# One ring of three PSUM banks for scores, diagonal blocks and turned maxima, drained by ScalarE, and value products of two steps back to back

## The chip, the cores and the metric

The kernel runs on one core of a Trainium2 chip. The metric is the device time of one execution, in microseconds (us). The engines are called TensorE (PE, with PEld for its weight loads), VectorE (DVE), ScalarE (ACT), GpSimd (POOL) and SyncE (SP, which starts most transfers).

## The reference, cut to what matters

A transformer block on 8 sequences of 1024 rows and 256 columns: a modulated layer norm, attention, a second modulated layer norm, and a feed-forward part whose operands are rounded to four bits in blocks of 16. The change touches attention alone:

```python
k_rec, v_rec = up-projections of latent_kv      # 16 heads of 16 columns
scores = einsum('bhqd,bhkd->bhqk', qh, k_rec) / sqrt(d)
scores = scores * exp(-0.01 * abs(q - k))       # a decay that depends on the distance
attn = softmax(scores, axis=-1)
out = einsum('bhqk,bhkd->bhqd', attn, v_rec)
```

The softmax subtracts each row's maximum of the decayed scores, so a maximum must be known before the exponentials are taken.

## The kernel before, in words

Four stages follow each other: setup, projection, attention (`attend_stage`, lines 494 to 985) and the feed-forward part. Projection leaves q and k in two scaled versions ("low" and "up"), each split into three bf16 parts, so that six bf16 terms stacked on 96 partitions make an exact enough fp32 product. Above the diagonal one version carries the decay, below it the other. The 128x128 block on the diagonal fits neither, and is made apart.

Attention works in 32 units, one for each sequence and group of four heads. A unit has 16 steps: `g // 8` is the half of the 1024 queries, `g % 8` the block of 128 keys. Everything is written out as one fixed order for each engine. Engines meet through counting semaphores.

TensorE, `unit_steps` (793 to 808), in each step:

- `scores` (744) four times, one for each head h: 128 keys by 512 queries. In a diagonal step (8 of 16: g = 0 to 3 and 12 to 15) the 128 queries of the diagonal block are left out, which leaves 384.
- Between them two tiles of `max_tile` (724), four matmuls: the scores of a later unit, 128 queries by 1024 keys, for the row maxima. The order in a step is S0, A first half, S1, A second half, B first half, S2, B second half, S3. Below, S0 to S3 are the score products and A and B the two tiles of a step; in the second step of a pair of steps the tiles are called C and D.
- After S1, where the next step is a diagonal one, `diagonals` (765): four 128x128 products into `side_ps`.
- At the end `values` (777) of the step two back (`LAG = 2`): four heads side by side in four column groups of 32 of the array, fp32, which the trace records as eight matmuls.
- After step 9, `turn_maxima` (737): two transposes of the maxima of the next unit, also into `side_ps`.

The maxima tiles have two buffers, `max_ps[:, i % 2]`, of two banks each. `bank_was_free` (565) lets the first half of tile i start when VectorE has finished tile i - 2. The scores have two banks, `score_ps[:, i % 2]`; `side_ps` and `pv_ps` have one each. That is all eight banks.

VectorE (`maxima`, 891) multiplies each tile with the decay and takes the row maximum, in one custom instruction and a short read of the result. In steps 7 and 8 it splits the maxima into three bf16 parts (901), in step 10 it copies the turned maxima (919). In the last two units it multiplies the diagonal block by its decay (927), reading `side_ps`.

ScalarE, `unit_steps` (860), takes the exponential of each score bank (`exp`, 839; on the diagonal steps with g % 4 of 1 or 2 over all 512 columns, those of the diagonal block among them). After h = 1 it takes the exponential of the diagonal block of the step before (`diagonal_exp`, 854), after h = 3 it copies the next diagonal block out of `side_ps` (`copy_diagonal`, 847), and twice a unit it copies the output (`copy_out`, 832). GpSimd multiplies the copied diagonal block by its decay (691) and subtracts the maxima (699). `probs` has four buffers, and `exp` of step g waits for `values` of step g - 4.

SyncE loads the operands of later units and waits for the events of this order (636).

Of the kernel before, what the change touches and what calls it, by code (L numbers as in the profile page):

```python
# [26 lines left out]
ALU = mybir.AluOpType  # L27
# [466 lines left out]
def attend_stage(nc, ctx, t, w):  # L494
# [12 lines left out]
    DIAG_EXP = 1  # L507
    LATE = UNITS * B - 2
# [6 lines left out]
    def sem(name):  # L515
# [27 lines left out]
    turned_max = side_ps[0:3 * UH * TILES, 0, 0:P // 2].bitcast(BF16)  # L543
    turned_whole = side_ps[0:UH * TILES, 1, :]
# [11 lines left out]
    max_turn_ready, max_turn_copied = sem("max_turn_ready"), sem("max_turn_copied")  # L556
    scores_ready, pv_done = sem("scores_ready"), sem("pv_done")
    diag_ready, diag_copied, diag_decayed, diag_shifted, diag_exp_done = (
        sem("diag_ready"), sem("diag_copied"), sem("diag_decayed"), sem("diag_shifted"), sem("diag_exp_done"))
    out_copied = sem("out_copied")  # L560
    out_stored = [sem(f"out_stored{i}") for i in range(OUTS)]
    maxima_done, exp_done = sem("maxima_done"), sem("exp_done")
    block = st.enter_context(nc.Block())

    def bank_was_free(eng, done, unit, per_unit, i):
# [19 lines left out]
    def tiles_of(b, u, g, last):  # L585

        later = 1 if g < STEPS // 2 else 2
        if last and later == 1 or isinstance(b, int) and UNITS * b + u + later >= UNITS * B:
            return None
        first = (g * PER_STEP + AHEAD) % MAX_TILES  # L590
        return (b, u + later, first) if u + later < UNITS else (b + 1, (u + later) % UNITS, first)

    @block.sync
    def _(sp):
# [41 lines left out]
        def step(unit):  # L636
            nonlast = unit < UNITS * B - 1
            if unit > 0:

                sp.wait_ge(exp_done, SCORE_TILES * unit)  # L640
                sp.wait_ge(diag_copied, 2 * DIAG * unit)
# [12 lines left out]
            if unit + 3 < UNITS * B:  # L654
                load_low((unit + 3) // UNITS, (unit + 3) % UNITS)
# [26 lines left out]
    @block.gpsimd  # L682
    def _(pool):
        for i in range(UNITS):
            nc.gpsimd.memset(low[1][i][KROWS:KROWS + 3], -1.0).then_inc(minus_ones_set, 1)
        for i in range(2):
            nc.gpsimd.memset(up[1][i][KROWS:KROWS + 3], -1.0).then_inc(minus_ones_set, 1)
        pool.wait_ge(const_loaded, 16)
        pool.wait_ge(minus_ones_set, UNITS + 2)

        def decay_diagonal(unit, g):
            n = diagonals_before(unit, g)
            pool.wait_ge(diag_copied, n + 1)
            if n > 0:
                pool.wait_ge(diag_shifted, n)
            nc.gpsimd.tensor_tensor(diag[:, g % 2], diag[:, g % 2], diag_decay[:].unsqueeze(1).broadcast_to([P, UH, P]),  # L696
                                    ALU.mult).then_inc(diag_decayed, 1)

        def shift_diagonal(unit, g):
            n, hf, at = diagonals_before(unit, g), g // TILES, g % DIAG * P  # L700
            pool.wait_ge(diag_copied if unit >= LATE else diag_decayed, n + 1)
            if n > 0:
                pool.wait_ge(diag_shifted, n)
            pool.wait_ge(shift_loaded[hf], 16 * (unit + 1))
            nc.gpsimd.tensor_tensor(diag[:, g % 2], diag[:, g % 2], shift[:, hf, :, at:at + P],  # L705
                                    ALU.subtract).then_inc(diag_shifted, 1)

        def unit_steps(unit):
            for g in range(DIAG):
                if unit < LATE:  # L710
                    decay_diagonal(unit, g)
                shift_diagonal(unit, g)
            for g in range(TILES + DIAG, STEPS):
                if unit < LATE:
                    decay_diagonal(unit, g)
                shift_diagonal(unit, g)

        for unit in range(UNITS * B):
            unit_steps(unit)
    @block.tensor  # L720
    def _(pe):
        pe.wait_ge(ident_ready, 1)

        def max_tile(b, u, i, half):
# [12 lines left out]
        def turn_maxima(unit):  # L737
            pe.wait_ge(max_parts_ready, 3 * (unit + 1))
            if unit > 0:
                pe.wait_ge(diag_copied, 2 * DIAG * unit - DIAG)  # L740
            pe.transpose(turned_max, max_parts[:].rearrange("p t n -> p (t n)"), ident_bf[:])
            pe.transpose(turned_whole, row_max[:, unit % 2], w["ident"][:]).then_inc(max_turn_ready, 1)

        def scores(b, u, g, h):

            hf, kb = g // TILES, g % TILES
            unit, i = UNITS * b + u, UH * g + h
# [6 lines left out]
            bank_was_free(pe, exp_done, unit, SCORE_TILES, i)  # L754
            if turn > q0:
                mm = pe.matmul(score_ps[:, i % 2, 0:turn - q0], up[1][u % 2][:, h, ks],  # L756
# [3 lines left out]
            if q1 > turn:  # L760
                mm = pe.matmul(score_ps[:, i % 2, turn - q0:HALF], low[1][u][:, h, ks],  # L761
                               low[0][u][:, h, turn:q1], start=True, stop=True)
            mm.then_inc(scores_ready, 1)

        def diagonals(b, u, g):
# [3 lines left out]
            if g == 0 and unit == 0 or g == TILES + DIAG and unit < UNITS * B - 1:  # L769
                pe.wait_ge(max_turn_copied, 2 * (unit + 1 + (g > 0)))  # L770
            pe.wait_ge(diag_copied, diagonals_before(unit, g))
            for h in range(UH):
                mm = pe.matmul(side_ps[:, h, :], low[1][u][0:KROWS, h, ks], low[0][u][0:KROWS, h, ks],  # L773
                               start=True, stop=True)
            mm.then_inc(diag_ready, 1)

        def values(b, u, g):
# [9 lines left out]
            pe.wait_ge(exp_done, SCORE_TILES * unit + UH * (g + 1))  # L787
# [5 lines left out]
        def unit_steps(b, u, first, last):  # L793
            unit = UNITS * b + u
            for g in range(STEPS):
# [9 lines left out]
                if not (first and g < LAG):  # L805
# [25 lines left out]
    def _(act):  # L831
# [7 lines left out]
        def exp(unit, g, h):  # L839
            i = UH * g + h  # L840
            first = P if is_diagonal(g) and g % DIAG == 0 else 0
            end = HALF - P if is_diagonal(g) and g % DIAG == DIAG - 1 else HALF
            act.wait_ge(scores_ready, SCORE_TILES * unit + i + 1)
            nc.scalar.activation(probs[:, g % PROBS, h, first:end], score_ps[:, i % 2, first:end],  # L844
                                 ACT.Exp).then_inc(exp_done, 1)

        def copy_diagonal(b, u, g):
            n = diagonals_before(UNITS * b + u, g)
            act.wait_ge(diag_ready, n + 1)
            if n >= 2:  # L850
                act.wait_ge(diag_exp_done, n - 1)
            nc.scalar.activation(diag[:, g % 2], side_ps[:], ACT.Copy).then_inc(diag_copied, 1)  # L852

        def diagonal_exp(b, u, g):
            unit, at = UNITS * b + u, g % DIAG * P
            act.wait_ge(exp_done, SCORE_TILES * unit + UH * (g + 1))
# [30 lines left out]
    def _(dve):  # L887
# [31 lines left out]
        def copy_turned(unit):  # L919
            dve.wait_ge(max_turn_ready, unit + 1)  # L920
            dve.wait_ge(max_rows_loaded, 16 * 6 * unit)
            if unit > 0:
                dve.wait_ge(max_stored, 16 * unit)
            nc.vector.tensor_copy(max_turned[:], turned_max).then_inc(max_turn_copied, 1)
            nc.vector.tensor_copy(max_whole[:], turned_whole).then_inc(max_turn_copied, 1)

        def decay_diagonal(b, u, g):
            n = diagonals_before(UNITS * b + u, g)
            dve.wait_ge(diag_ready, n + 1)
            dve.wait_ge(diag_exp_done, n - 1)  # L930
            nc.vector.tensor_tensor(diag[:, g % 2], side_ps[:], diag_decay[:].unsqueeze(1).broadcast_to([P, UH, P]),  # L931
                                    ALU.mult).then_inc(diag_copied, 1)
# [6 lines left out]
        def round_weights(step):  # L939

            pieces = len(weights) * QUANT_STEPS
            for n in range(pieces * step // FREE_STEPS, pieces * (step + 1) // FREE_STEPS):
                if n == 0:
                    dve.wait_ge(weights_loaded, 16 * 5)
                    dve.wait_ge(exp_done, SCORE_TILES * (UNITS * (B - 1) + 1))
                    dve.wait_ge(diag_copied, 2 * DIAG * (UNITS * (B - 1) + 1))
# [5 lines left out]
        def unit_steps(b, u, last):  # L952
            unit = UNITS * b + u
            following = (b, u + 1) if u < UNITS - 1 else (b + 1, 0)
            for g in range(STEPS):
                ahead = tiles_of(b, u, g, last)
                for i in range(PER_STEP):
# [4 lines left out]
                    if not last and (g, i) == (10, 0):  # L962
                        copy_turned(unit + 1)
# [9 lines left out]
        copy_turned(0)  # L973
# [713 lines left out]
```

## Time and profile before

| | us |
|---|---|
| median of 3 runs | 2623.03 (2622.95 to 2626.25) |
| the profiled execution, its own time | 2628.24 |
| its span, first to last instruction | 2626.4 |
| busy TensorE, matmuls | 2451.9 (93%) |
| busy VectorE | 2078.3 (79%) |
| busy ScalarE | 1840.8 (70%) |
| busy GpSimd | 1290.8 (49%) |

The span is the time from the first to the last instruction on the core. The execution's own time is 1.8 us longer. A matmul's record reaches from its start to its modelled end, and matmuls overlap in the array, so TensorE looks busier than it is: the pitch from one start to the next tells its speed, not the length of a record. A record followed by "x2" covers two instructions. In brackets behind a record stands how long the engine sat idle before it and what released it.

### The profile page before, as it was taken

How to read it: one execution, taken by the hardware profiler on the slowest of the kernel's cores; microseconds unless marked ns; L12 is line 12 of the kernel's file. 1: busy time of each engine (PE TensorE's matmuls, PEld its weight loads, DVE VectorE, ACT ScalarE, POOL GpSimd, SP SyncE). 2: the span in 40 equal slices, each digit the busy share in tenths (PEclk: the TensorE clock that was granted, in tenths of full speed). 3: DMA queues.
4: the chain of work that ended last, by engine and by line, in shares of the span. 5: the costliest groups of instructions: out<-in, count | busy, mean ns of one | idle time of the engine just before them, and what ended most of it. 6: DMA issues, size and time to landing. Idle time of an engine off the chain costs nothing. (4 is left out here: it accounts for less than half of the span.)

```text
span 2626.4 us, 40901 instructions
## 1 busy us (share of the span) xinstructions
PE 2451.9 (93%) x12710; PEld 1034.0 (39%) x12710; DVE 2078.3 (79%) x3876; ACT 1840.8 (70%) x3608; POOL 1290.8 (49%) x1107
## 2 busy tenths in 40 slices
PE   5878759999999999999999999999886999999998
PEld 3333312333333333333333333333223666666665
DVE  5988878888888888888888888888755787888875
ACT  3666605888888888888888888888743555555554
POOL 3656642535435344353453543534314677777774
PEclk9677757999999999999999999999986999999999
DMA  4777884756647557466474564755302112212110
GB/s 151 240 249 246 266 162 133 149 117 138 142 97 159 120 122 159 98 142 138 110 163 105 137 143 98 162 117 113 88 25 66 51 57 57 57 55 57 57 45 18
DMA packets 273769, 315.54 MB, mean 120 GB/s; under 512 B 38032, under 2 KB 182160, under 8 KB 273424
## 3 DMA queue, kind: packets, MB, share of 16 engines
q1 hardware_dynamic: 264336, 304.54, 48.1%
q10 hardware_dynamic: 9216, 8.39, 0.9%
q8 instruction: 102, 1.67, 0.3%
q14 instruction: 115, 0.94, 0.1%
HBM read 225.78 MB, written 85.46 MB: 119 GB/s over the span
## 5 line engine op out<-in xcount | busy, mean ns | idle before, releaser
L897 DVE CUSTOM_DVE_ANT_0 unread<-max_ps,toeplitz_sb 128x1024 bf16<-128x1024 f32 x1024 | 1219.6, 1222 | 263.8 <-PE max_ps L732 260.0
L844 ACT ACTIVATE probs<-score_ps 128x512 f32<-128x512 f32 (+1 forms) x2048 | 1074.5, 589 | 207.7 <-PE score_ps L761 122.2
L732 PE MATMUL max_ps<-k_low,q_low 96*128 96x512 bf16 x2048 | 719.7, 393 | 27.4 <-DVE ident_bf L888 17.9
L696 POOL TENSOR_TENSOR diag<-diag,diag_decay 128x512 f32<-128x512 f32 x240 | 305.1, 1271 | 840.6 <-ACT diag L852 828.0
L789 PE MATMUL pv_ps<-probs,v 128*32 128x512 f32 x4096 | 546.9, 606 | 0.0
L756 PE MATMUL score_ps<-q_up,k_up 99*128 99x512 bf16 (+3 forms) x1280 | 411.1, 322 | 14.3 <-ACT probs L844 13.4
L761 PE MATMUL score_ps<-q_low,k_low 99*128 99x512 bf16 (+3 forms) x1280 | 406.6, 319 | 6.1 <-ACT probs L844 5.0
L705 POOL TENSOR_TENSOR diag<-diag,shift 128x512 f32<-128x512 f32 x256 | 334.1, 1305 | 86.0 <-DVE diag L931 66.1
L1335 PE MATMUL gu_ps<-wgu_t,turned 128*128 128x512 f32 (+1 forms) x768 | 316.3, 562 | 0.8 <-DVE hid L1550 0.8
L756 PEld LDWEIGHTS score_ps<-q_up,k_up 99*128 99x128 bf16 x1280 | 123.2, 97 | 458.9 <-ACT probs L844 434.0
L732 PEld LDWEIGHTS max_ps<-k_low,q_low 96*128 96x128 bf16 x2048 | 197.5, 98 | 188.0 <-DVE row_max L897 86.6
L348 POOL TENSOR_TENSOR parts<-rest,parts 128x512 bf16<-128x512 f32 x128 | 173.7, 1376 | 105.9 <-ACT parts L463 104.3
L761 PEld LDWEIGHTS score_ps<-q_low,k_low 99*128 99x128 bf16 x1280 | 124.5, 98 | 248.9 <-ACT probs L844 183.0
L852 ACT ACTIVATE diag<-side_ps 128x512 f32<-128x512 f32 x240 | 154.1, 642 | 73.9 <-PE side_ps L773 73.9
L1335 PEld LDWEIGHTS gu_ps<-wgu_t,turned 128*128 128x128 f32 x768 | 142.4, 192 | 142.4 <-issue 124.4
L1308 PE MATMUL fdown_ps<-wd_g,hid_t 128*128 128x256 f32 (+1 forms) x768 | 190.5, 390 | 4.8 <-DVE y_out L1570 3.9
L858 ACT ACTIVATE probs<-diag 128x512 f32<-128x512 f32 x256 | 171.1, 668 | 0.2 <-POOL diag L705 0.2
L1308 PEld LDWEIGHTS fdown_ps<-wd_g,hid_t 128*128 128x128 f32 (+1 forms) x768 | 141.4, 191 | 44.8 <-issue 21.8
L1360 ACT ACTIVATE turned<-fturn_ps 128x256 f32<-128x256 f32 x64 | 24.6, 384 | 177.3 <-PE fturn_ps L1325 177.3
L1550 DVE TENSOR_TENSOR hid<-gu_ps,silu 128x704 f32<-128x704 f32 x64 | 57.1, 892 | 110.6 <-ACT silu L1400 110.6
L789 PEld LDWEIGHTS pv_ps<-probs,v 128*32 128x32 f32 x4096 | 80.8, 108 | 123.2 <-issue 110.1
L305 DVE TENSOR_TENSOR rest<-full,parts 128x512 f32<-128x512 f32 x128 | 116.8, 922 | 15.6 <-ACT parts L459 9.4
(154 smaller groups left out, 2845.5 us busy)
## 6 DMA issues: line engine op xcount, KB each, us to landing
shift<-max_whole_dram SPq DMA_DIRECT2D x64, 1024.0 KB, 7.6
splits<-parts SPq DMA_DIRECT2D x128, 384.0 KB, 2.7
q_low<-splits SPq DMA_DIRECT2D x192, 128.0 KB, 7.1
k_low<-splits SPq DMA_DIRECT2D x192, 128.0 KB, 8.3
q_up<-splits SPq DMA_DIRECT2D x192, 128.0 KB, 9.3
k_up<-splits SPq DMA_DIRECT2D x192, 128.0 KB, 10.2
v_padded<-v_out SPq DMA_DIRECT2D x64, 256.0 KB, 3.7
v<-v_padded SPq DMA_DIRECT2D x32, 512.0 KB, 12.1
```

Source lines behind the costliest of these rows:

```text
L348: nc.gpsimd.tensor_tensor(parts[:, n % RING, 2, :], rest[:, n % RING, :], parts[:, n % RING, 1, :], ALU.subtract).then_inc(low_ready, 1)
L696: nc.gpsimd.tensor_tensor(diag[:, g % 2], diag[:, g % 2], diag_decay[:].unsqueeze(1).broadcast_to([P, UH, P]), ALU.mult).then_inc(diag_dec ...
L705: nc.gpsimd.tensor_tensor(diag[:, g % 2], diag[:, g % 2], shift[:, hf, :, at:at + P], ALU.subtract).then_inc(diag_shifted, 1)
L732: mm = pe.matmul(max_ps[:, i % 2, half * HALF:(half + 1) * HALF], low[0][u][0:KROWS, h, qb * P:(qb + 1) * P], low[1][u][0:KROWS, h, half * ...
L756: mm = pe.matmul(score_ps[:, i % 2, 0:turn - q0], up[1][u % 2][:, h, ks], up[0][u % 2][:, h, q0:turn], start=True, stop=True)
L761: mm = pe.matmul(score_ps[:, i % 2, turn - q0:HALF], low[1][u][:, h, ks], low[0][u][:, h, turn:q1], start=True, stop=True)
L789: mm = pe.matmul(pv_ps[h * VW:(h + 1) * VW, :], v[u % 2][:, kb, h, :], probs[:, g % PROBS, h, :], start=(kb == 0), stop=(kb == TILES - 1))
L844: nc.scalar.activation(probs[:, g % PROBS, h, first:end], score_ps[:, i % 2, first:end], ACT.Exp).then_inc(exp_done, 1)
L858: nc.scalar.activation(probs[:, g % PROBS, :, at:at + P], diag[:, g % 2], ACT.Exp).then_inc(diag_exp_done, 1)
L897: nc.vector.tensor_tensor_reduce(unread[:, i % 2, :], max_ps[:, i % 2, :], toeplitz[:, at:at + S], 1.0, -3.0e38, ALU.mult, ALU.max, row_ma ...
L1308: mm = pe.matmul(down_ps[:, 0:D], hid_t[i % 2][0:rows, c, :], w["wd_g"][0:rows, b, c, :], start=(c == 0), stop=(c == IC - 1))
L1335: mm = pe.matmul(gu_ps[:, c:min(c + HALF, GU)], turned[i % 2][:, k, :], w["wgu_t"][:, k, c:min(c + HALF, GU)], start=(k == 0), stop=(k == ...
```

## The change

One ring of three banks, `score_ps[:, at % 3]`, takes the place of the two score banks and of `side_ps`. `ring_order` lists everything that passes through it: the turned maxima of a unit, the diagonal blocks and the scores, in TensorE's order. `ring_ready` counts what TensorE has filled, `ring_drained` what ScalarE has emptied. A write to the ring waits for the entry three before it. ScalarE now drains every entry: it copies the diagonal block after h = 1, not after h = 3, and in the last two units too; it copies the turned maxima after step 9, in place of VectorE; its exponential in diagonal steps leaves the diagonal block out, as two instructions where that block lies inside; and it copies the output after h = 0 of steps 2 and 10, not after steps 1 and 9. On TensorE the value products of two steps stand together at the end of each odd step. The maxima tiles, their two buffers and their place between the scores are as before.

```diff
-    score_ps = st.enter_context(nc.psum_tensor("score_ps", [P, 2, HALF], F32))
-    side_ps = st.enter_context(nc.psum_tensor("side_ps", [P, UH, P], F32))
+    score_ps = st.enter_context(nc.psum_tensor("score_ps", [P, RING, HALF], F32))
...
+    def ring_order():
+        yield "turn", 0
+        yield "diagonal", 0, 0
+        for unit in range(UNITS * B):
+            for g in range(STEPS):
+                for h in range(UH):
+                    yield "score", unit, g, h
+                    if h == 1 and g < STEPS - 1 and is_diagonal(g + 1):
+                        yield "diagonal", unit, g + 1
+                    if h == 1 and g == STEPS - 1 and unit < UNITS * B - 1:
+                        yield "diagonal", unit + 1, 0
+                if g == 9 and unit < UNITS * B - 1:
+                    yield "turn", unit + 1
...
     @block.tensor
+        def ring_free(*tile):
+            at = ring_at[tile]
+            if at >= RING:
+                pe.wait_ge(ring_drained, at - RING + 1)
+            return at % RING
...
         def scores(b, u, g, h):
-            bank_was_free(pe, exp_done, unit, SCORE_TILES, i)
+            slot = ring_free("score", unit, g, h)
...
         def diagonals(b, u, g):
-            pe.wait_ge(diag_copied, diagonals_before(unit, g))
+            slot = ring_free("diagonal", unit, g)
...
         def values(b, u, g):
-            pe.wait_ge(exp_done, SCORE_TILES * unit + UH * (g + 1))
+            pe.wait_ge(ring_drained, ring_at["score", unit, g, UH - 1] + 1)
...
-                if not (first and g < LAG):
+                if g % 2 == 1 and not (first and g < LAG):
+                    values(*steps_back(b, u, g, LAG + 1))
                     values(*steps_back(b, u, g, LAG))
...
     @block.scalar
         def exp(unit, g, h):
-            first = P if is_diagonal(g) and g % DIAG == 0 else 0
-            end = HALF - P if is_diagonal(g) and g % DIAG == DIAG - 1 else HALF
+            block = g % DIAG * P
+            pieces = [(0, block), (block + P, HALF)] if is_diagonal(g) else [(0, HALF)]
+            act.wait_ge(ring_ready, at + 1)
+            for first, end in pieces:
+                if first < end:
+                    op = nc.scalar.activation(probs[:, g % PROBS, h, first:end], score_ps[:, at % RING, first:end],
+                                              ACT.Exp)
+            op.then_inc(ring_drained, 1)
...
         def copy_diagonal(b, u, g):
+            act.wait_ge(ring_ready, at + 1)
             if n >= 2:
                 act.wait_ge(diag_exp_done, n - 1)
...
+        def copy_turned(unit):
+            nc.scalar.activation(max_turned[:], bank[0:3 * UH * TILES, 0:P // 2].bitcast(BF16),
+                                 ACT.Copy).then_inc(max_turn_copied, 1)
+            nc.scalar.activation(max_whole[:], bank[0:UH * TILES, P:2 * P], ACT.Copy).then_inc(max_turn_copied, 1)
+            act.wait_ge(max_turn_copied, 2 * (unit + 1))
+            act.sem_inc(ring_drained, 1)
...
                 for h in range(UH):
                     exp(unit, g, h)
+                    if h == 0 and g == 2 and not first:
+                        copy_out(unit - 1, 1)
+                    if h == 0 and g == TILES + 2:
+                        copy_out(unit, 0)
                     if h == DIAG_EXP and not (first and g == 0) and is_diagonal((g - 1) % STEPS):
                         diagonal_exp(*steps_back(b, u, g, 1))
-                if is_diagonal((g + 1) % STEPS) and unit + (g == STEPS - 1) < LATE:
-                    copy_diagonal(*steps_on(b, u, g))
-                if g == 1 and not first:
-                    copy_out(unit - 1, 1)
-                if g == TILES + 1:
-                    copy_out(unit, 0)
+                    if h == 1 and is_diagonal((g + 1) % STEPS) and not (last and g == STEPS - 1):
+                        copy_diagonal(*steps_on(b, u, g))
+                if g == 9 and not last:
+                    copy_turned(unit + 1)
...
     @block.vector
         def decay_diagonal(b, u, g):
-            nc.vector.tensor_tensor(diag[:, g % 2], side_ps[:], diag_decay[:].unsqueeze(1).broadcast_to([P, UH, P]),
-                                    ALU.mult).then_inc(diag_copied, 1)
+            nc.vector.tensor_tensor(diag[:, g % 2], diag[:, g % 2], diag_decay[:].unsqueeze(1).broadcast_to([P, UH, P]),
+                                    ALU.mult).then_inc(late_decayed, 1)
```

## Rows read from the trace of the kernel before

**Rows 1.** The page: its first line.

```profile
span 2626.4 us, 40901 instructions
```

**Rows 2.** Windows: engines' busy us (instructions), PEclk, DMA share, GB/s.

```profile
1015.10:1062.50 47.40, 46.95 (x307) 15.81 (x305) 38.79 (x71) 40.74 (x82) 20.41 (x16) 1.00 0.60 130
1868.50:1920.00 51.50, 41.77 (x260) 11.80 (x258) 30.16 (x31) 40.27 (x80) 13.86 (x8) 0.97 0.18 51
```

**Rows 3.** Waits of the whole span: us in total, times, longest.

```profile
PEld score_ps L756 <- ACT probs L844: 434.0, 829, 1.7
...
PEld max_ps L732 <- DVE row_max L897: 86.6, 169, 1.5
```

**Rows 4.** Timeline of one ordinary step: start, length, engine, line, operation.

```profile
1000.12 0.39 PE L756 MATMUL score_ps<-q_up,k_up 99*128 99x512 bf16 x1
...
1000.61 2.16 ACT L844 ACTIVATE probs<-score_ps 128x512 f32<-128x512 f32 x4 [0.37 <-PE score_ps L756]
...
1000.78 0.59 PE L732 MATMUL max_ps<-k_low,q_low 96*128 96x512 bf16 x2
1001.25 0.10 PEld L756 LDWEIGHTS score_ps<-q_up,k_up 99*128 99x128 bf16 x1 [0.36 <-ACT probs L844]
...
1001.31 1.22 DVE L897 CUSTOM_DVE_ANT_0 unread<-max_ps,toeplitz_sb 128x1024 bf16<-128x1024 f32 x1 [0.57 <-PE max_ps L732]
...
1001.75 0.39 PE L756 MATMUL score_ps<-q_up,k_up 99*128 99x512 bf16 x1
...
1002.07 1.06 PE L789 MATMUL pv_ps<-probs,v 128*32 128x512 f32 x8
...
1002.46 1.22 DVE L897 CUSTOM_DVE_ANT_0 unread<-max_ps,toeplitz_sb 128x1024 bf16<-128x1024 f32 x1
...
1003.07 0.39 PE L756 MATMUL score_ps<-q_up,k_up 99*128 99x512 bf16 x1
```

**Rows 5.** Timeline: a maxima tile that waits for VectorE.

```profile
1005.75 1.22 DVE L897 CUSTOM_DVE_ANT_0 unread<-max_ps,toeplitz_sb 128x1024 bf16<-128x1024 f32 x1
...
1007.04 0.10 PEld L732 LDWEIGHTS max_ps<-k_low,q_low 96*128 96x128 bf16 x1 [0.48 <-DVE row_max L897]
```

**Rows 6.** Timeline of PEld at attention's end, where value products follow each other.

```profile
1932.55 0.13 PEld L789 LDWEIGHTS pv_ps<-probs,v 128*32 128x32 f32 x4 [0.30 <-ACT probs L858]
1932.98 0.13 PEld L789 LDWEIGHTS pv_ps<-probs,v 128*32 128x32 f32 x4 [0.30 <-issue]
```

**Rows 7.** Timeline: the split of the maxima, and the transposes of two units.

```profile
1010.21 1.22 DVE L897 CUSTOM_DVE_ANT_0 unread<-max_ps,toeplitz_sb 128x1024 bf16<-128x1024 f32 x1 [0.41 <-PE max_ps L732]
...
1011.56 1.22 DVE L897 CUSTOM_DVE_ANT_0 unread<-max_ps,toeplitz_sb 128x1024 bf16<-128x1024 f32 x1
...
1014.90 0.26 PE L741 MATMUL side_ps<-ident_bf,max_parts 128*96 128x128 bf16 x1
...
1062.44 0.26 PE L741 MATMUL side_ps<-ident_bf,max_parts 128*96 128x128 bf16 x1
```

**Rows 8.** Timeline of TensorE in diagonal steps 13 and 14 of a unit.

```profile
1024.80 0.59 PE L732 MATMUL max_ps<-k_low,q_low 96*128 96x512 bf16 x2
...
1027.10 0.28 PE L756 MATMUL score_ps<-q_up,k_up 99*128 99x256 bf16 x1
...
1027.66 0.59 PE L732 MATMUL max_ps<-k_low,q_low 96*128 96x512 bf16 x2
```

**Rows 9.** Timeline of ScalarE in diagonal steps, and one output copy.

```profile
1028.54 0.68 ACT L858 ACTIVATE probs<-diag 128x512 f32<-128x512 f32 x1
1029.06 1.14 ACT L844 ACTIVATE probs<-score_ps 128x512 f32<-128x512 f32 x2
1030.02 0.68 ACT L852 ACTIVATE diag<-side_ps 128x512 f32<-128x512 f32 x1
1030.49 0.96 ACT L844 ACTIVATE probs<-score_ps 128x384 f32<-128x384 f32 x2
...
1039.10 0.63 ACT L837 ACTIVATE out_t<-pv_ps 128x512 f32<-128x512 f32 x1
```

More of the change, by code:

```diff
@@ L507, in attend_stage @@
     DIAG_EXP = 1
+    RING = 3
     LATE = UNITS * B - 2
@@ L555, in attend_stage, with ring_order_table @@
         sem("max_scores_ready"), sem("max_parts_ready"), sem("max_rest_ready"))
[L556 to L559, printed above, removed]
+    max_turn_copied = sem("max_turn_copied")
+    ring_ready, ring_drained, pv_done = sem("ring_ready"), sem("ring_drained"), sem("pv_done")
+    diag_decayed, late_decayed, diag_shifted, diag_exp_done = (
+        sem("diag_decayed"), sem("late_decayed"), sem("diag_shifted"), sem("diag_exp_done"))
     out_copied = sem("out_copied")
     out_stored = [sem(f"out_stored{i}") for i in range(OUTS)]
-    maxima_done, exp_done = sem("maxima_done"), sem("exp_done")
+    maxima_done = sem("maxima_done")
     block = st.enter_context(nc.Block())
+    def ring_order_table():
+        return {tile: i for i, tile in enumerate(ring_order())}
     def bank_was_free(eng, done, unit, per_unit, i):
@@ L638, in step @@
             if unit > 0:
-                sp.wait_ge(exp_done, SCORE_TILES * unit)
-                sp.wait_ge(diag_copied, 2 * DIAG * unit)
+                sp.wait_ge(ring_drained, ring_at["score", unit, 0, 0])
                 load_shift(unit, 1)
@@ L692, in decay_diagonal @@
             n = diagonals_before(unit, g)
-            pool.wait_ge(diag_copied, n + 1)
+            pool.wait_ge(ring_drained, ring_at["diagonal", unit, g] + 1)
             if n > 0:
@@ L700, in shift_diagonal @@
             n, hf, at = diagonals_before(unit, g), g // TILES, g % DIAG * P
-            pool.wait_ge(diag_copied if unit >= LATE else diag_decayed, n + 1)
+            if unit < LATE:
+                pool.wait_ge(diag_decayed, n + 1)
+            else:
+                pool.wait_ge(late_decayed, n - 2 * DIAG * LATE + 1)
             if n > 0:
@@ L738, in turn_maxima @@
             pe.wait_ge(max_parts_ready, 3 * (unit + 1))
[L739 to L742, printed above, removed]
+            bank = score_ps[:, ring_free("turn", unit), :]
+            pe.transpose(bank[0:3 * UH * TILES, 0:P // 2].bitcast(BF16),
+                         max_parts[:].rearrange("p t n -> p (t n)"), ident_bf[:])
+            pe.transpose(bank[0:UH * TILES, P:2 * P], row_max[:, unit % 2], w["ident"][:]).then_inc(ring_ready, 1)
         def scores(b, u, g, h):
             hf, kb = g // TILES, g % TILES
-            unit, i = UNITS * b + u, UH * g + h
+            unit = UNITS * b + u
             if g == 0 and h == 0:
@@ L839, in exp @@
         def exp(unit, g, h):
-            i = UH * g + h
-            first = P if is_diagonal(g) and g % DIAG == 0 else 0
-            end = HALF - P if is_diagonal(g) and g % DIAG == DIAG - 1 else HALF
-            act.wait_ge(scores_ready, SCORE_TILES * unit + i + 1)
-            nc.scalar.activation(probs[:, g % PROBS, h, first:end], score_ps[:, i % 2, first:end],
-                                 ACT.Exp).then_inc(exp_done, 1)
+            at = ring_at["score", unit, g, h]
+            block = g % DIAG * P
@@ new lines, in copy_turned @@
+        def copy_turned(unit):
+            at = ring_at["turn", unit]
+            bank = score_ps[:, at % RING, :]
+            act.wait_ge(ring_ready, at + 1)
+            if unit > 0:
+                act.wait_ge(max_rows_loaded, 16 * 6 * unit)
+                act.wait_ge(max_stored, 16 * unit)
+            nc.scalar.activation(max_turned[:], bank[0:3 * UH * TILES, 0:P // 2].bitcast(BF16),
[3 more added lines that the diff above has]
+            act.sem_inc(ring_drained, 1)
@@ L854, in diagonal_exp @@
         def diagonal_exp(b, u, g):
             unit, at = UNITS * b + u, g % DIAG * P
-            act.wait_ge(exp_done, SCORE_TILES * unit + UH * (g + 1))
+            act.wait_ge(ring_drained, ring_at["score", unit, g, UH - 1] + 1)
             act.wait_ge(diag_shifted, diagonals_before(unit, g + 1))
@@ L961, in unit_steps @@
                         split_maxima(*following, SPLIT_AT.index((g, i)))
-                    if not last and (g, i) == (10, 0):
-                        copy_turned(unit + 1)
                 if is_diagonal((g + 1) % STEPS) and LATE <= unit + (g == STEPS - 1) < UNITS * B:
```

37 lines of the change are left out of this document (12 added, 25 removed).

## The prediction, before the changed kernel was run

> **What bounds the kernel now.** I read the page's first line and its table of slices, then the windows, the waits, and the timeline of one unit, engine by engine. The span is 2626.4 us [rows 1] and the execution's own time 2628.24. Attention is over half of it. From the transposes of one unit (1014.90) to those of the next (1062.44) are 47.54 us [rows 7], for 16 steps, or 2.97 us a step. In such a unit TensorE shows 46.95 busy of 47.40 us, VectorE 38.79, ScalarE 40.74, and the granted clock is 1.00, the 2.4 GHz level [rows 2]. The waits name ScalarE: weight loads of score products waited 434.0 us for it, in 829 pieces, and those of maxima tiles only 86.6 us for VectorE, in 169 [rows 3]. That list misleads. A weight load may sit idle while the array still works, so the pitch of the matmuls has to be read.
>
> Rows 4 give an ordinary step. S0 starts at 1000.12, A's second half at 1000.78 after three pitches of 0.22, S3 at 1001.75, the value products at 1002.07, and the next S0 at 1003.07: 2.95 us. Eight pitches of 0.22 are 1.74, and the value products take 1.00. What is left is 0.21: 0.10 between S3 and the value products (0.32 where a pitch is 0.22) and some 0.10 in which S2 and S3 wait for ScalarE. S2's weights load at 1001.25, 0.64 after the exponential of S0 began (1000.61) [rows 4]. So TensorE is the bound, with small losses at two places.
>
> **What the change saves.** A value step is two passes on four column groups at once. At attention's end, where they follow one another, the passes are 0.43 apart (1932.55, 1932.98) [rows 6], so a value step inside a run costs 0.86, not the 1.00 + 0.10 of one that stands alone. Per pair of steps the change saves 0.24, and with the third bank S2 and S3 wait no more: 2 x 0.10. TensorE alone would need 16 x 0.215 + 0.10 + 1.00 + 0.86 = 5.40 us per pair in place of 5.90.
>
> The Trainium skill (TensorEngine Tiling (Array Packing), Key Properties) says that changing the tiling mode, not just the tile, drains TensorE. The trace agrees with 0.24 per stay in the narrow mode. By that rule alone the change is a gain; that result is the first rival below.
>
> **What the change costs: the maxima tiles.** They keep two buffers, and every step still makes two of them, but TensorE now makes none for 1.86 us on end. Follow one pair of steps with tiles A, B (even step) and C, D (odd step). VectorE starts on A 0.53 after A's second half started (1000.78, 1001.31) and on B 1.15 later (1002.46) [rows 4]. TensorE may write into B's buffer, with D, 1.29 after VectorE began on B: VectorE at 1005.75, the waiting weight load at 1007.04 [rows 5]. So D starts no sooner than 0.53 + 1.15 + 1.29 = 2.97 us after A's second half. Queued behind D on TensorE are S2, D's second half, S3, both value products, then S0, A's first half, S1, and A's second half of the next pair: 3 x 0.22, 0.32, 1.00 + 0.86, 3 x 0.22 = 3.49 us [rows 4, 6]. The loop closes at 2.97 + 3.49 = 6.46 us per pair. No buffer of the ring enters it. Before, the same loop spans two steps, but D's successors up to the next A hold one value step, not two: 2.97 + 2.63 = 5.60, under the 5.90 that TensorE needed. It was hidden by 0.30; now it leads by 1.06 over the 5.40. C finds its own wait too (A's buffer, 0.53 + 1.29), but D's wait comes later and covers it.
>
> In diagonal steps the score products are shorter and four small products are added. From A's second half (1024.80) to B's first half is 0.22, from there to the next S0 (1027.10) 2.08, from S0 to A's second half (1027.66) 0.56 [rows 8]. With the second value step: 2.97 + 2.08 + 0.86 + 0.56 = 6.47. The same number, so I use 6.46 for all eight pairs of a unit: 51.7 us. Step 8 splits the maxima between A and B, where VectorE starts 1.35 apart (1010.21, 1011.56) [rows 7] and not 1.15: +0.2. The transposes after step 9 stand in the chain: at most their 0.26 [rows 7], I take 0.2. Step 3 has no diagonal product (-0.2) and step 11 has one beside full scores (+0.1). Together 52.0.
>
> **What the change costs: ScalarE.** In ordinary pairs it has eight exponentials of 0.52 (four in 2.16, the last of 0.6 [rows 4]) in 6.46 us, and three filled banks when the value products start. It waits, and nobody waits for it. In diagonal steps its pitches are 0.48 for a 512 exponential (two from 1029.06 to 1030.02), some 0.09 less for 384 columns, 0.52 for the diagonal exponential, 0.47 for the copy [rows 9]. One thing is new there: the copy of the next diagonal block now stands right behind the diagonal exponential of the step before, and waits for just that one (same buffer). It loses the overlap, 0.68 + 0.05 in place of 0.52, or 0.2 per diagonal step. Where is ScalarE last? In pair 2, 3. From S0 of step 2: exponential at 0.49, output copy 0.97, exponential 1.44, diagonal exponential 1.92, copy 2.6, exponentials 3.07 and 3.55. S0 of step 3 needs the copy's bank: 2.6 + 0.64 = 3.24. C follows at 3.41, S1 needs the next bank at 3.71, and D comes at 4.10, where VectorE would have let it go at 0.56 + 2.97 = 3.53. That is +0.6. Pair 10, 11 has ScalarE's copies of the turned maxima (two, and a wait for both before the bank is given back) and the output copy: a late bank for S0 and S1 of step 11, +0.2. Bounds for these copies: 0, if they run where ScalarE would stand idle anyway, and twice the 0.68 of a diagonal copy [rows 9], 1.4, of which D's later wait covers some 1.1. Pair 14, 15: +0.1. Sum 0.9.
>
> The exponential in two pieces has no row. Sixteen of them a unit. From below: two pieces read 384 columns in place of 512, and 128 columns cost 0.09, so -0.05 if a second piece is free but for its start. From above: a whole second instruction less its overlap, 0.68 - 0.52 = 0.16 more [rows 9], and up to +0.2. I take 0, next to the lower end, since start overhead hides in the pitch of 0.48 against lengths of 0.57. At +0.2, the eight pieces in pairs 2, 3 and 14, 15 lie on the chain: +1.6 per unit.
>
> The Trainium skill (ScalarE: Activation LUTs, What ACT_TABLE_LOAD costs) has 186 ns + 0.833 ns per column for an ACTIVATE with immediates, with 93 ns of overlap. By it, as an estimate, the two pieces cost 0.51 and the single one 0.52, so the sum would stay.
>
> **Moves that cost nothing.** VectorE loses the copy of the turned maxima and gains nothing before the last two units. The output copies come after their value products (end of steps 1 and 9) and ahead of the next ones that overwrite `pv_ps` (steps 3 and 11), 4 us later. GpSimd's decay and subtraction get their block earlier, and it is busy 20.41 of 47.40 us [rows 2]. SyncE's waits are on the same events by another count. The exponential of step g needs the value products of g - 4; these end in the pair just ahead of S0, which TensorE issues after them anyway, so PROBS hides it.
>
> **Sum.** A unit goes from 47.5 to 52.0 + 0.9 = 52.9: +5.4. Maxima tiles are made during 30.5 of 32 units (unit 30 stops half-way): +165. In the last 1.5 units, without tiles, ordinary pairs gain 0.4 (six of them) and diagonal pairs lose 0.7, since ScalarE takes over copies from VectorE: +2. Against the profiled execution: 2628.2 + 167 = 2795. The median of the runs shown lies 5.2 below that execution, so I forecast 2790.
>
> **Rivals.**
> (a) The pairing pays: VectorE does not gate, and TensorE's own order holds. Per unit four ordinary pairs gain 0.5 and four diagonal ones some 0.25, or 3 us; times 32 that is -95: 2530. For it: TensorE is busy 99% of the unit [rows 2], and the waits blame ScalarE's banks five times more than VectorE [rows 3]. Against it: it decides only if the loop of 6.46 falls under 5.90, which needs 0.56 less in rows that are measured (VectorE's 1.15 pitch, the 1.29 of rows 5). Chance 0.08.
> (b) The change does nothing, because the loop costs just what the drains gave: 2623. It needs a loop of 5.9. Chance 0.02.
> (c) Same loop, but ScalarE's pieces cost a full instruction: +1.6 x 30.5 = 49 on top: 2840. For it: ScalarE is close behind TensorE in diagonal steps, back to back from 1028.54 to past 1030.49 [rows 9]. Chance 0.16.
> (d) The clock. TensorE will stand still for a seventh of each pair. In 1868.50 to 1920.00, where it was busy 41.77 of 51.50 us, the granted clock was still 0.97 [rows 2]. Were it so throughout, 3% of time at half speed adds at most 0.03 x 5.4 us a pair, +40 in all: 2830. Chance 0.05.
> (e) The forecast: 0.69.
>
> **Chances and range.** What a measurement can tell from no change is 0.2%, 5 us. Slower is (c), (d), (e): 0.90; same 0.02; faster 0.08. The floor of the range is the tile loop without ScalarE's 0.9 per unit (-27) and with a second value step 0.03 cheaper (-7): 2755. The top is (c): 2840.
>
> **What would show it.** Of after: ordinary pairs 6.46 apart, from S0 of an even step to the next. Waits of the maxima tiles on VectorE (L732 on L897's result) up from 86.6 to some 250 us and more, those of score products on ScalarE in ordinary steps gone. VectorE's idle time in front of A, released by TensorE, near 1.8 us once a pair. Value products as 16 records in some 1.9 us. The diagonal copy some 0.7 behind the diagonal exponential. Pair 2, 3 the longest, near 6.9. A unit of 52 to 53 us. The prediction is wrong if D's first half starts less than 1.2 us after VectorE began on B, if a pair of value products takes much under 1.86, or if units come at 47 or less.

## The result, and the profile after

| | before | after |
|---|---|---|
| median of 4 runs, us | 2624.64 | 2788.20 (2785.77 to 2792.88) |
| ratio | | 1.0623 (95% interval 1.0604 to 1.0642) |
| span of the profiled execution | 2626.4 | 2791.1 |
| one unit of attention | 47.54 (most units 47.39) | 52.59 |

The forecast was 2790 (2755 to 2840), slower with 0.90. Experiments are given by the median of four executions and the ratio of their fast ones, which leaves out one execution of e7 (3606.45 us at a granted clock of 0.638, the others 2991.53 to 2999.06 at 0.92) and one of e9 (2934.70).

The page of after: its first line and the group of VectorE's maxima instruction (busy, mean ns | idle before it). The second fence has its waits, as in [rows 3].

```profile
span 2791.1 us, 41397 instructions
...
L943 DVE CUSTOM_DVE_ANT_0 unread<-max_ps,toeplitz_sb 128x1024 bf16<-128x1024 f32 x1024 | 1210.6, 1222 | 437.8 <-PE max_ps L759 430.0
```

```profile
DVE unread L943 <- PE max_ps L759: 430.0, 337, 2.0
PEld max_ps L759 <- DVE row_max L943: 268.2, 382, 1.5
...
PEld score_ps L783 <- ACT probs L872: 160.7, 369, 0.9
...
PEld score_ps L783 <- ACT diag L881: 118.1, 128, 1.1
```

TensorE's loads of maxima tiles now wait 268.2 us for VectorE, against 86.6 [rows 3], and VectorE idles 430.0 us for TensorE. Each waits for the other in turn, which is what a loop through both looks like. What TensorE's loads wait for ScalarE's exponentials fell, from 434.0 [rows 3] to 160.7 on the same line of code. That line has a new wait of 118.1 us, for the copy of the diagonal block, which now comes through the ring.

The timeline of after shows one ordinary pair (TensorE, VectorE), and the transposes of two units:

```profile
1007.48 0.59 PE L759 MATMUL max_ps<-k_low,q_low 96*128 96x512 bf16 x2
...
1008.01 1.23 DVE L943 CUSTOM_DVE_ANT_0 unread<-max_ps,toeplitz_sb 128x1024 bf16<-128x1024 f32 x1 [1.22 <-PE max_ps L759]
...
1009.15 1.22 DVE L943 CUSTOM_DVE_ANT_0 unread<-max_ps,toeplitz_sb 128x1024 bf16<-128x1024 f32 x1
...
1009.30 0.39 PE L759 MATMUL max_ps<-k_low,q_low 96*128 96x512 bf16 x1 [0.35 <-DVE row_max L943]
...
1010.44 0.39 PE L759 MATMUL max_ps<-k_low,q_low 96*128 96x512 bf16 x1 [0.32 <-DVE row_max L943]
...
1011.42 1.92 PE L814 MATMUL pv_ps<-probs,v 128*32 128x512 f32 x16
...
1013.27 0.39 PE L783 MATMUL score_ps<-q_up,k_up 99*128 99x512 bf16 x1
...
1013.94 0.60 PE L759 MATMUL max_ps<-k_low,q_low 96*128 96x512 bf16 x2
...
1014.46 1.23 DVE L943 CUSTOM_DVE_ANT_0 unread<-max_ps,toeplitz_sb 128x1024 bf16<-128x1024 f32 x1 [1.79 <-PE max_ps L759]
...
1026.39 0.26 PE L767 MATMUL score_ps<-ident_bf,max_parts 128*96 128x128 bf16 x1
...
1078.98 0.26 PE L767 MATMUL score_ps<-ident_bf,max_parts 128*96 128x128 bf16 x1
```

A's second half starts at 1007.48, VectorE begins on A at 1008.01 (+0.53) and on B at 1009.15 (+1.14). C waits for A's buffer (1009.30, VectorE's start on A + 1.29), D for B's (1010.44, again + 1.29). The value products start at 1011.42 and take 1.85 up to the next S0. A's second half of the next pair is at 1013.94: 6.46 us after the last one. VectorE stood idle for 1.79 before the next A.

### The profile page after: what moved, and what is told of

Its sections match the earlier page's. It is cut to its first block and busy times, and to the rows that moved or that the text cites. A ratio compares the mean times of both kernels' runs of the same rounds, so it can differ in the third digit from the quotient of the medians.

```text
span 2791.1 us, 41397 instructions
## 1 busy us (share of the span) xinstructions
PE 2453.9 (88%) x12710; PEld 1065.4 (38%) x12710; DVE 2061.6 (74%) x3812; ACT 1841.2 (66%) x4200; POOL 1286.7 (46%) x1107
## 5 line engine op out<-in xcount | busy, mean ns | idle before, releaser
L872 ACT ACTIVATE probs<-score_ps 128x512 f32<-128x512 f32 (+3 forms) x2560 | 1016.0, 485 | 316.4 <-PE score_ps L788 195.0
L759 PE MATMUL max_ps<-k_low,q_low 96*128 96x512 bf16 x2048 | 746.4, 393 | 109.9 <-DVE row_max L943 86.3
L814 PE MATMUL pv_ps<-probs,v 128*32 128x512 f32 x4096 | 499.4, 606 | 0.0
L783 PE MATMUL score_ps<-q_up,k_up 99*128 99x512 bf16 (+3 forms) x1280 | 399.0, 321 | 86.9 <-ACT diag L881 71.9
L788 PE MATMUL score_ps<-q_low,k_low 99*128 99x512 bf16 (+3 forms) x1280 | 400.0, 318 | 20.5 <-ACT probs L872 18.6
L759 PEld LDWEIGHTS max_ps<-k_low,q_low 96*128 96x128 bf16 x2048 | 195.0, 98 | 368.8 <-DVE row_max L943 268.2
L783 PEld LDWEIGHTS score_ps<-q_up,k_up 99*128 99x128 bf16 x1280 | 123.8, 97 | 348.9 <-ACT probs L872 160.7
L814 PEld LDWEIGHTS pv_ps<-probs,v 128*32 128x32 f32 x4096 | 107.9, 110 | 234.5 <-issue 185.1
L881 ACT ACTIVATE diag<-score_ps 128x512 f32<-128x512 f32 x256 | 153.0, 598 | 40.1 <-PE score_ps L798 19.5
```

The lines of the kernel that those rows point to most:

```text
L759: mm = pe.matmul(max_ps[:, i % 2, half * HALF:(half + 1) * HALF], low[0][u][0:KROWS, h, qb * P:(qb + 1) * P], low[1][u][0:KROWS, h, half * ...
L783: mm = pe.matmul(score_ps[:, slot, 0:turn - q0], up[1][u % 2][:, h, ks], up[0][u % 2][:, h, q0:turn], start=True, stop=True)
L788: mm = pe.matmul(score_ps[:, slot, turn - q0:HALF], low[1][u][:, h, ks], low[0][u][:, h, turn:q1], start=True, stop=True)
L814: mm = pe.matmul(pv_ps[h * VW:(h + 1) * VW, :], v[u % 2][:, kb, h, :], probs[:, g % PROBS, h, :], start=(kb == 0), stop=(kb == TILES - 1))
L872: op = nc.scalar.activation(probs[:, g % PROBS, h, first:end], score_ps[:, at % RING, first:end], ACT.Exp)
```

## The experiments

All ratios are to the kernel before, run on the same chip. I name pairs by their first step.

### e1: the ring, single value steps

```diff
-                if g % 2 == 1 and not (first and g < LAG):
-                    values(*steps_back(b, u, g, LAG + 1))
+                if not (first and g < LAG):
                     values(*steps_back(b, u, g, LAG))
```

> The changed kernel with one value step at the end of each step again; the ring, the pieces and ScalarE's copies stay. Theory (the two maxima buffers and the pair of value products make the loop of 6.46 us): the loop over two steps falls to 5.60 and hides under TensorE; ordinary steps lose their waits for ScalarE and come at 2.82 to 2.87 us in place of 2.94; diagonal steps pay 0.1 for the copy behind the diagonal exponential. About 2605, between 2590 and 2625. Rival (the ring of three or ScalarE's new work is what costs): it stays near 2788.

Measured: 2595.42, ratio 0.988 (0.9864 to 0.9897). With the ring in place, pairing costs 193 us (2788.20 against 2595.42). The rest of the change gains 31. An ordinary step of e1, from S0 to S0:

```profile
1034.80 0.39 PE L783 MATMUL score_ps<-q_up,k_up 99*128 99x512 bf16 x1
...
1036.33 0.38 PE L783 MATMUL score_ps<-q_up,k_up 99*128 99x512 bf16 x1
1036.64 1.07 PE L814 MATMUL pv_ps<-probs,v 128*32 128x512 f32 x8
1037.64 0.39 PE L783 MATMUL score_ps<-q_up,k_up 99*128 99x512 bf16 x1
```

2.84 us, with S3 at 1.53 and no wait: TensorE's own order. Six of the eight diagonal steps come at 2.85 to 2.88 too, so the copy behind the diagonal exponential cost next to nothing there, where I had expected 0.1. The others are step 2 with the output copy (3.37, see e8) and step 3 (2.63), which has no diagonal product.

### e2: pairing alone, in the kernel before

```diff
-                if not (first and g < LAG):
+                if g % 2 == 1 and not (first and g < LAG):
+                    values(*steps_back(b, u, g, LAG + 1))
                     values(*steps_back(b, u, g, LAG))
```

> The kernel before with the pairing of the value products alone: two score banks, side_ps and the old order of ScalarE stay. Theory: ordinary pairs come 6.46 us apart, the whole near 2785, up to 2810 because the output copies now wait for the pair. Rival (pairing pays where the ring does not spoil it): 2530 to 2600.

Measured: 2802.55, ratio 1.0674 (1.0658 to 1.069). Value products of e2:

```profile
1039.52 1.92 PE L789 MATMUL pv_ps<-probs,v 128*32 128x512 f32 x16
...
1045.99 1.92 PE L789 MATMUL pv_ps<-probs,v 128*32 128x512 f32 x16
```

The pair costs 6.47 with two score banks and no ring, and the whole is 176 us slower than the kernel before on its chip. With e1 this settles the cause from both sides: pairing alone makes it slower, everything but pairing makes it faster.

### e3 and e4: the maxima tiles at other places

```diff
 e3
-                for h, halves in enumerate(((0,), (1, 2), (3,), ())):
+                for h, halves in enumerate(((0, 1), (), (2, 3), ())):
 e4
+                for h, halves in enumerate(((0, 1), (), (), (2, 3)) if g % 2 == 1 else ((0, 1), (), (2, 3), ())):
```

> The changed kernel with the maxima tiles at other places of a step: both halves of the first tile after S0, both of the second after S2. Behind D's first half, up to A's second half of the next pair, stand two score products fewer. Theory: the loop is 2.97 + 0.43 + 0.32 + 1.86 + 0.43 = 6.01 us, ordinary pairs come 6.01 apart in place of 6.46; in diagonal pairs ScalarE limits part of the gain; total 2700 (2680 to 2720). Rival (ScalarE's ring limits the pair): no change, 2788.

> As the kernel with the tiles apart, but in odd steps both halves of D after S3, right ahead of the value products. Theory: the tile loop is 2.97 + 0.22 + 0.32 + 1.86 + 0.43 = 5.80 us; now the ring's own loop is as long: S3 of the odd step waits for the exponential three entries back and starts 3.21 after S0, then D 0.43, 0.32, 1.86: 5.82. Ordinary pairs 5.8 apart, diagonal pairs no better than with the tiles apart or up to 0.3 worse; total 2670 to 2710. Rival as there: 2788.

Measured: e3 2752.00, ratio 1.0481 (1.0466 to 1.0497); e4 2797.16, ratio 1.0653 (1.0637 to 1.0669). Ordinary pairs of e3, then of e4:

```profile
1050.26 1.93 PE L814 MATMUL pv_ps<-probs,v 128*32 128x512 f32 x16
...
1056.27 1.07 PE L814 MATMUL pv_ps<-probs,v 128*32 128x512 f32 x8
```

```profile
1017.33 1.93 PE L814 MATMUL pv_ps<-probs,v 128*32 128x512 f32 x16
...
1023.14 1.06 PE L814 MATMUL pv_ps<-probs,v 128*32 128x512 f32 x8
```

6.01 and 5.81, each the number that the loop gives. Both totals missed (2700 and 2670 to 2710), because three of the four diagonal pairs got longer. Pairs 14, 0 and 2 take 6.78, 6.66 and 6.79 in e3 and 7.00, 6.94 and 7.01 in e4, where after has 6.47, 6.47 and 6.73. Only pair 12 got shorter (5.94 and 6.22 in place of 6.47). In e4 the clock adds some 13 us: eight units hold a short stretch at a granted clock of 0.50 (1.2 GHz) and take 54.14 where the others take 52.50. What ends the waits in the longer pairs is ScalarE's copy of the diagonal block, so ScalarE's ring looks like the longest loop there. No run varied it in these two kernels. Pair 2 of e3, ScalarE and TensorE:

```profile
1041.05 0.66 ACT L901 ACTIVATE probs<-diag 128x512 f32<-128x512 f32 x1
...
1041.80 0.60 ACT L881 ACTIVATE diag<-score_ps 128x512 f32<-128x512 f32 x1
...
1042.45 0.34 PE L783 MATMUL score_ps<-q_up,k_up 99*128 99x384 bf16 x1 [0.86 <-ACT diag L881]
```

The copy starts 0.75 after the diagonal exponential, and the product that needs its bank 0.65 after that.

### e5, e6, e9, e10: a longer VectorE pitch

```diff
             nc.vector.tensor_tensor_reduce(...
...
                                           row_max[:, u % 2, i:i + 1]).then_inc(maxima_done, 1)
+            if count > 1:
+                dve.wait_ge(pad_done, count - 1)
+            nc.vector.tensor_copy(pad[:], w["ident"][:]).then_inc(pad_done, 1)      # e5, e6
+            nc.vector.tensor_tensor(pad[:], w["ident"][:], w["ident"][:], ALU.add).then_inc(pad_done, 1)   # e9, e10
```

> The changed kernel with an added VectorE copy (128x128, unused) behind each maxima instruction, which lengthens the pitch from one tile to the next by d, to be read from the trace (about 0.2 us); a buffer is given back as early as before. Theory: VectorE's pitch from A to B stands in the loop once per pair, so each ordinary pair grows by d, to 6.46 + d, and the whole by some 7 of 8 pairs x 30.5 units x d: about 2830 for d = 0.2. Rival (TensorE's order or ScalarE's ring sets the pair, VectorE is busy 74% and has room): 2788 to 2795.

> The same added copy in the kernel before. Theory: its tile loop of 5.60 + d = 5.80 us over two steps stays under the 5.90 at which two steps come, so the time does not move: 2624 to 2632. Rival (VectorE matters to both alike): +40 us or more, as in the changed kernel.

> As the changed kernel with the slower VectorE, but the added instruction is a 128x128 add and not a copy. In the run with the copy, ordinary pairs grew by the 0.14 us that the copy took and diagonal ones more, where the copy lasted up to the end of a GpSimd instruction. Theory: an add does not wait for GpSimd; its pitch d is 0.15 to 0.25; every pair that VectorE leads grows by d, and the whole by d x 7.5 x 30.5: 2822 to 2845, at 2834 for d = 0.2. Rival (the time of the copy run came from VectorE's load in general): 2865 again.

> The added 128x128 add in the kernel before. Theory: its tile loop of 5.60 + d over two steps stays under 5.90, in diagonal steps nearly level with 5.72: 2624 to 2640. Rival (VectorE's load costs before as well): 2718 again, as with the copy.

Measured: e5 2864.75 (1.0911, 1.0893 to 1.093), e6 2718.39 (1.0356, 1.0341 to 1.0372), e9 2903.52 (1.1038, 1.0993 to 1.1082), e10 2729.28 (1.0397, 1.0381 to 1.0413). As totals, all four expectations failed. In ordinary steps the theory holds to 0.01. Value products of e9 in an ordinary pair, then of e10 in an ordinary step:

```profile
1083.18 1.92 PE L815 MATMUL pv_ps<-probs,v 128*32 128x512 f32 x16
...
1089.85 1.50 PE L815 MATMUL pv_ps<-probs,v 128*32 128x512 f32 x12
```

```profile
1045.19 1.07 PE L790 MATMUL pv_ps<-probs,v 128*32 128x512 f32 x8
...
1048.13 1.06 PE L790 MATMUL pv_ps<-probs,v 128*32 128x512 f32 x8
```

6.67 is 6.46 plus 0.20, by which the add lengthens VectorE's pitch (1.35 in place of 1.15). In e5 the pair takes 6.59, and the copy lengthens the pitch by 0.14. The kernel before stays at 2.94: its tile loop has that much room. At a granted clock of 1.00, diagonal pairs 14 and 0 of e5 and e9 grew by the same 0.14 and 0.20.

The totals missed for two reasons. The first is that in diagonal steps some of the added instructions lasted up to the end of one of GpSimd's. In e5 and e9 this shows in pair 12 alone, which takes 7.59 and 7.66 where the longer pitch gives 6.61 and 6.67. That is some 30 us over the 30 units. In e6 and e10 it shows in most diagonal steps. VectorE of e6, then GpSimd of e6:

```profile
1020.39 1.19 DVE L903 COPY pad<-ident_sb 128x128 f32<-128x128 f32 x1
...
1022.64 0.30 DVE L903 COPY pad<-ident_sb 128x128 f32<-128x128 f32 x1
```

```profile
1020.22 1.27 POOL L697 TENSOR_TENSOR diag<-diag,diag_decay 128x512 f32<-128x512 f32 x1 [0.98 <-ACT diag L853]
1021.57 1.28 POOL L706 TENSOR_TENSOR diag<-diag,shift 128x512 f32<-128x512 f32 x1
```

The copy that takes 0.22 alone took 1.19, up to 0.09 after the end of GpSimd's instruction (1021.49). The next one took only 0.30 beside the next GpSimd instruction. I took an add to be free of this. It isn't: in e10 it took 0.27 to 1.26.
The second reason is the clock. In the profiled execution of e9, 16 units took 56.55 to 58.03 us and nearly all others 54.98. The long ones hold stretches at a granted clock of 0.50. That is some 42 us of its 2907.41, and some 9 us in e5. So these four runs test the theory in ordinary steps and in diagonal pairs 14 and 0, and not by their totals.

### e7 and e11: a ring of two

```diff
-    RING = 3
+    RING = 2
```

> The changed kernel with a ring of two banks. Theory: the ring is in no loop of an ordinary pair (with two banks, S3 of the odd step could start 3.73 after S0, and it starts at 4.28), so ordinary pairs stay at 6.46; diagonal pairs, with ten entries through two banks and the copy behind the diagonal exponential, go to 7.5 to 8.5, and the whole to 2900 to 3020. Rival (the ring's length is what ties ordinary pairs): they lengthen too, to 7 and more.

> The ring with single value steps, but of two banks. Theory: an ordinary step of the kernel before, 2.95, was the loop through its two score banks, exponential and score product in turn (0.49 + 0.52 + 0.64 + 0.32 + 1.00 = 2.97), not TensorE's own order (2.82); so ordinary steps go from 2.85 back to 2.95. Diagonal blocks now share the two banks: 3.6 to 4.1 per diagonal step; the whole 2820 to 2930. Rival (the third bank is worth nothing in ordinary steps): they stay at 2.85.

Measured: e7 2996.64, ratio 1.141 (1.139 to 1.1429); e11, the same in e1, 2883.84, ratio 1.0984 (1.0965 to 1.1004). Both totals are within what was expected. An ordinary pair and a diagonal pair of e7, then an ordinary step of e11:

```profile
1019.88 1.92 PE L814 MATMUL pv_ps<-probs,v 128*32 128x512 f32 x16
...
1026.34 1.06 PE L814 MATMUL pv_ps<-probs,v 128*32 128x512 f32 x8
...
1047.92 1.92 PE L814 MATMUL pv_ps<-probs,v 128*32 128x512 f32 x16
...
1055.84 0.64 PE L814 MATMUL pv_ps<-probs,v 128*32 128x512 f32 x4
```

```profile
1043.68 1.06 PE L814 MATMUL pv_ps<-probs,v 128*32 128x512 f32 x8
...
1046.63 0.64 PE L814 MATMUL pv_ps<-probs,v 128*32 128x512 f32 x4
```

The ordinary pair keeps its 6.46 with one bank fewer: the ring is not in the loop that sets it. Diagonal pairs go to 7.30 (pair 12), 7.92 (14), 7.80 (0) and a median of 8.10 (2), against the 7.5 to 8.5 expected. The single step goes from 2.84 back to 2.95, the step of the kernel before. Its diagonal steps are 3.33 to 4.44 where 3.6 to 4.1 was expected, and 2.63 in step 3.

### e8: single value steps, three buffers for the diagonal block

```diff
-    diag = sb("diag", [P, 2, UH, P], F32)
+    diag = sb("diag", [P, 3, UH, P], F32)
...
-                if g % 2 == 1 and not (first and g < LAG):
-                    values(*steps_back(b, u, g, LAG + 1))
+                if not (first and g < LAG):
...
-            if n >= 2:
-                act.wait_ge(diag_exp_done, n - 1)
+            if n >= 3:
+                act.wait_ge(diag_exp_done, n - 2)
```

> The ring of three with one value step per step, and three buffers for the copied diagonal block in place of two, so that the copy no longer waits for the diagonal exponential right ahead of it. Theory: diagonal steps at 2.85 us are TensorE's, the 0.2 of ScalarE shows only beside the output copy in step 2: 0.2 to 0.4 us per unit, 2588 (2580 to 2593) against 2595. Rival (the added wait costs in every diagonal step, 8 x 0.2 per unit): 2545.

Measured: 2588.00, ratio 0.9855 (0.9841 to 0.987). Like e1 it beats both kernels. The gain is where it was expected: with the output copy in step 2, value steps come 3.25 apart in place of 3.37, and the other diagonal steps stay at 2.85 to 2.86. It is smaller than expected: a unit takes 46.41 in place of 46.56, or 0.15 less and not 0.2 to 0.4. Over 30 units that is 4.5 of the 7.6 us between the two spans. Another 3.0 lie behind attention, where the edit changes nothing.

## Why the prediction was right

**The tile loop.** 6.46 per ordinary pair was forecast, 6.46 measured, and each term with it: 0.53, 1.14, 1.29 and the stretch from D to the next A. Taking two or three score products out of that stretch (e3, e4) or lengthening VectorE's pitch (e9) moved the pair by what was added or taken. Diagonal pairs were forecast at 6.47 before ScalarE's part, and three of four came at 6.47. Step 8's split cost 0.20 (pair 8 at 6.66), as forecast; the transposes, ScalarE's copies and the diagonal product of step 11 cost 0.41 (pair 10 at 6.87), against 0.2 + 0.2 + 0.1.

**ScalarE.** Pair 2 was forecast at 6.9 and came at 6.73. The mechanism is the one described. ScalarE and TensorE of after:

```profile
1054.03 0.57 ACT L872 ACTIVATE probs<-score_ps 128x256 f32<-128x256 f32 x2
...
1054.45 0.66 ACT L901 ACTIVATE probs<-diag 128x512 f32<-128x512 f32 x1
...
1055.20 0.60 ACT L881 ACTIVATE diag<-score_ps 128x512 f32<-128x512 f32 x1
...
1055.85 0.34 PE L783 MATMUL score_ps<-q_up,k_up 99*128 99x384 bf16 x1 [0.86 <-ACT diag L881]
```

The diagonal exponential to the copy is 0.75, where 0.73 was said, and the bank comes back 0.65 later. The sizes that were off: two pieces of an exponential take 0.42 (1054.03 to 1054.45), the lower end of the bounds and not the 0.48 that I took (the estimate beside it had 0.51), and pair 14 showed none of the 0.1. Rival (c) falls with it. A unit came to 52.59, not 52.9.

**The end of attention.** I had +2 for the last 1.5 units. From the last transposes to the last output copy before went 66.7 us (1868.3 to 1935.0), after 75.9 (2024.6 to 2100.5): +9.2. The 30 units between the first and the last transposes behind step 9 gave 5.13 each, 154.0 of the 164.7 us by which the span grew. Most of the 9.2 is rival (d), the clock, which in after's attention showed here and nowhere else. Two windows of after, then value pairs there:

```profile
2045.00:2052.30 7.30, 5.88 (x41) 1.88 (x41) 6.63 (x6) 5.36 (x14) 4.50 (x3) 0.87 0.39 144
...
2059.00:2066.70 7.70, 6.81 (x25) 1.36 (x24) 7.49 (x7) 4.59 (x11) 0.32 (x1) 0.67 0.00 0
```

```profile
2044.96 2.88 PE L814 MATMUL pv_ps<-probs,v 128*32 128x512 f32 x16
...
2066.72 1.92 PE L814 MATMUL pv_ps<-probs,v 128*32 128x512 f32 x16
...
2072.00 1.92 PE L814 MATMUL pv_ps<-probs,v 128*32 128x512 f32 x16
```

The pair at 2044.96 took 2.88 in place of 1.92: the clock there was 0.50 up to 2046.9 and 1.00 from then on. How much the clock cost can be read from runs whose last units hold the same instructions in the same order. From the last transposes to the last output copy e9 took 73.2 us at a mean granted clock of 0.91, and after 75.9 at 0.87. Three pairs that after ran at 0.68 to 0.76 and e9 at 0.94 to 1.00 took 7.16, 8.33 and 7.72 against 5.63, 6.63 and 5.78, which is 5.2 us. On the other side e6, with the last units of the kernel before, took 65.7 at 1.00, and before 66.7 at 0.97. So the clock is at least 4.2 of the 9.2. Going on in proportion from 0.87 and 0.91 to 1.00, after would take 67 to 68 us, about 2 more than e6. That is an estimate, and it agrees with the +2 of the forecast. The term left out was the clock, by the same estimate some 7 us.

The nearness of 2788 to 2790 is in part luck: 30 units grew by 154.0 where 30 x 5.4 = 162 was forecast, and the clock at the end, which the sum did not have, gave most of that back. Without it the time would still lie inside the range.

**What was read wrong.** I wrote that TensorE bounds the kernel before, with small losses at two places. It does not. Before, in the last unit, without a maxima tile:

```profile
1903.35 1.06 PE L789 MATMUL pv_ps<-probs,v 128*32 128x512 f32 x8
...
1906.29 1.07 PE L789 MATMUL pv_ps<-probs,v 128*32 128x512 f32 x8
```

Four matmuls fewer per step, and still 2.94. The step is the loop through two score banks: exponential 0.49 after S0, the next 0.52 later, S3 0.64 after that, the value products 0.32 and 1.00 later: 2.97. The waits for ScalarE that I set aside as misleading named the bound, by a narrow margin over TensorE's 2.84. e11 shows it from the other side. With three banks and no tiles, e1's steps are 2.46 apart (1870.41 to 1875.33 for two), and 0.49 + 0.64 + 0.32 + 1.00 is 2.45. The error cost the forecast nothing, since the tile loop is longer than either.

```profile
1870.41 1.07 PE L814 MATMUL pv_ps<-probs,v 128*32 128x512 f32 x8
...
1872.88 1.06 PE L814 MATMUL pv_ps<-probs,v 128*32 128x512 f32 x8
...
1875.33 1.06 PE L814 MATMUL pv_ps<-probs,v 128*32 128x512 f32 x8
```

It does change what pairing is worth. Rival (a) priced a gain from spared drains. In the same tile-free stretch after has a pair every 5.28 (2066.72, 2072.00), and e1 two single steps in 4.92. Even without the maxima tiles, bunching the value products loses to spreading them, because ScalarE's ring then stands still too: ScalarE sits idle 1.25 us before S0's exponential of that pair, and the later score products wait for its exponentials. The 0.24 a pair that the prediction took for spared drains is there (1.85 for two value steps in a row, 1.00 for each alone, and 0.10 ahead of either), and it decides nothing here.

## What to carry to other kernels

Before work of one kind is bunched on an engine, follow each loop through a double buffer once around: consumer's pitch, release, everything queued behind the waiting instruction up to the next fill. Bunching puts twice the block into one turn of every such loop, and here the one that set the pace was a loop whose buffers the change had left alone. To see whether an engine or a loop sets a step, look for a stretch in which the engine has less to do and the step is as long.

## What the runs showed of the hardware that I had not expected

- A 128x128 add or copy on VectorE from SBUF, 0.22 to 0.29 us alone, took up to 1.26 (e10) and 1.19 (e6) beside a GpSimd instruction of 1.27 that reads SBUF, while the maxima instruction, with one input in PSUM, kept its 1.20 to 1.23 (e10).
- Beside a memset of GpSimd, which only writes SBUF, the copy and the add part ways: ahead of attention, where GpSimd sets `k_low` and `k_up`, four copies of e6 took 3.36 to 3.50 us and held up the maxima instruction behind them, and every add of e10 took 0.29.
- In after the granted clock was 1.00 through a unit in which TensorE was busy 46.77 of 52.60 us. In e9, with 85 to 86 of 100 us busy, it was 0.93 to 1.00 over stretches of 100 us from 500 to 2100 (1.00 is the level of 2.4 GHz), and its runs spread from 2883.50 to 2934.70, more than the 7 us of after.

```profile
1026.40:1079.00 52.60, 46.77 (x311) 16.81 (x308) 38.25 (x68) 40.61 (x100) 20.40 (x16) 1.00 0.49 117
```
